# A transformer block: query and key rows packed two heads to a load, written to DRAM once and repeated by 18 small transfers a quad

## What is computed

```
x = x + attn(layernorm(x), w_attn, w_proj, embk, embv)
q, k, v = split(x @ w_attn)                      # 16 heads, d = 8
rel = tril(idx[:, None] - idx[None, :]);  rk = embk[rel];  rv = embv[rel]
att = einsum('bhtd,bhsd->bhts', q, k) / sqrt(d) + einsum('bhtd,tsd->bhts', q, rk)
att = softmax(where(causal, att, -inf))
y = einsum('bhts,bhsd->bhtd', att, v) + einsum('bhts,tsd->bhtd', att, rv)
x = x + y @ w_proj
x = x + moe_ffn(layernorm(x), ...)
```

## Time and profile before

| | |
|---|---|
| median of 3 runs | 943.62 us (940.1 to 944.53) |
| profiled execution, its own time | 949.27 us |
| its span | 947.7 us |
| PE, DVE, ACT, POOL busy | 76%, 64%, 56%, 28% |
| granted TensorE clock, mean | 0.923 |
| first stage, to the first exponential | 111.84 us |
| DMA | 141.37 MB, 149 GB/s mean |

### The profile page before, as it was taken

One profiled execution on the slowest core, in us unless ns is written; L12 is line 12 of the kernel. 1 busy time (PEld: TensorE's weight loads), 2 busy tenths in 40 slices (PEclk: granted clock), 3 DMA queues, 4 the chain that ended last, 5 costly groups with the idle time before them and its releaser, 6 DMA issues. The chain is left out here.

```text
span 947.7 us, 27167 instructions
## 1 busy us (share of the span) xinstructions
PE 717.4 (76%) x10380; PEld 513.2 (54%) x10380; DVE 605.8 (64%) x1930; ACT 529.3 (56%) x1106; POOL 262.4 (28%) x252
## 2 busy tenths in 40 slices
PE   3552277787777887787887787888319999799997
PEld 2331155566565665665666655666216666466664
DVE  4822267685767685766686767777245767647776
ACT  3442278676768575767586777776064334243342
POOL 9411044343334442334452335443000000000000
PEclk9766599999999899999899999999659999999999
DMA  9598758767658776668767659642320000000000
GB/s 303 187 259 255 200 178 267 207 174 206 179 186 263 206 191 177 169 188 241 229 189 193 184 177 262 202 146 74 88 91 1 12 12 12 12 1 11 11 11 11
DMA packets 115675, 141.37 MB, mean 149 GB/s; under 512 B 7088, under 2 KB 81248, under 8 KB 115552
## 3 DMA queue, kind: packets, MB, share of 16 engines
q1 hardware_dynamic: 115552, 139.72, 50.4%
HBM read 82.81 MB, written 56.89 MB: 147 GB/s over the span
## 5 line engine op out<-in xcount | busy, mean ns | idle before, releaser
L801 ACT ACTIVATE work<-ps,nmin 128x128 f32<-128x128 f32 (+3 forms) x512 | 250.0, 537 | 135.2 <-DVE nmin L862 101.3
L862 DVE CUSTOM_DVE_ANT_0 ps<-ps,near 128x128 f32<-128x128 f32 (+3 forms) x512 | 242.5, 509 | 91.7 <-PE ps L683 63.5
L695 PE MATMUL ps<-ident,work 128*128 128x128 f32 x1280 | 213.6, 286 | 80.5 <-ACT work L790 75.4
L695 PEld LDWEIGHTS ps<-ident,work 128*128 128x128 f32 x1280 | 142.3, 144 | 118.3 <-ACT work L790 103.0
L847 DVE COPY work<-ps 128x512 f32<-128x512 f32 (+1 forms) x192 | 123.4, 643 | 86.7 <-PE ps L695 78.5
L683 PE MATMUL ps<-qkb 128*128 128x128 bf16 (+3 forms) x512 | 129.3, 305 | 35.2 <-ACT work L801 32.0
L652 POOL TENSOR_SCALAR_AFFINE_SELECT work<-work 128x512 f32<-128x512 f32 x96 | 61.1, 636 | 330.2 <-ACT work L790 314.0
L656 POOL TENSOR_TENSOR work<-work 128x512 f32<-128x512 f32 x96 | 124.5, 1297 | 8.0
L1219 ACT ACTIVATE silu<-h_ps 128x512 f32<-128x512 f32 x80 | 47.8, 597 | 134.3 <-PE h_ps L1182 134.1
L1194 PEld LDWEIGHTS y_ps<-w_sb,hT 128*128 128x128 f32 x640 | 82.6, 191 | 35.4 <-issue 30.6
L712 PE MATMUL ps<-work,vb 128*9 128x128 f32 x2560 | 96.2, 278 | 6.7 <-ACT relS L779 6.0
(11 more groups left out here) (104 smaller groups left out, 690.8 us busy)
## 6 DMA issues: line engine op xcount, KB each, us to landing
near<-w_slots SPq DMA_DIRECT2D x96, 512.0 KB, 4.6
w_slots<-relS SPq DMA_DIRECT2D x128, 256.0 KB, 4.3
qk_rows<-work SPq DMA_DIRECT2D x48, 256.0 KB, 4.4
qkb<-qk_rows SPq DMA_DIRECT2D x32, 384.0 KB, 5.7
near<-w_slots SPq DMA_DIRECT2D x32, 256.0 KB, 5.0
w_slots<-near SPq DMA_DIRECT2D x8, 512.0 KB, 5.8
v_dram<-work SPq DMA_DIRECT2D x4, 576.0 KB, 6.1
vb<-v_dram SPq DMA_DIRECT2D x4, 576.0 KB, 5.8
```

The costliest lines, as they stand in the source:

```text
L695: ins = nc.tensor.transpose(tp_ps[:, m % 2, n * P:(n + 1) * P], prob[:, m % PROBS, n * P:(n + 1) * P], ident[:, :])
L801: ins = nc.scalar.activation(prob[:, m % PROBS, h * wide:(h + 1) * wide], qk_ps[:, m % 3, h * wide:(h + 1) * wide], ACT.Exp, bias=nmin[:, ...
L862: nc.vector.tensor_tensor_reduce(out=scores, in0=scores, in1=near[:, q % NEAR, a, 4 * P - wide:4 * P, r], scale=1.0, scalar=3e38, op0=ALU. ...
```

## The change

The parts are written once each: `qk_rows` has 3 entries, 6 transfers a group in place of 12. The tile `qkb` becomes two: `qb` (a column block for each head; even heads have their 48 rows on partitions 0 to 47, odd heads on 64 to 111, zeros elsewhere) and `kb` (one column block for a pair of heads, one head in each half). A head's product takes its `qb` against the pair's `kb`. `load_qk` repeats the parts: for each of the two sides 3 transfers for q (24, 16 and 8 partitions) and 6 for k (8 partitions each), all of 2 heads x 1 KB a partition: 18 a quad, 384 KB in all as before.

In the first stage the groups overlap: PE turns the next group ahead of the values of this one, the values go to banks of their own (`value_banks`), ACT copies the next group's turned rows early, layernorm statistics are `bn_stats`/`bn_aggr` for three groups ahead. Group 0's values stay on the chip. Five of eight masks are issued later, quads 4 to 7 are loaded before the rows of group 2, and `wait_rows` moves from ACT's and SP's way into the main loop to the first use of the memory in question (SP's `load_v`, POOL's second row tile, ACT's first `av_copy`).

```diff
-Q_PART = [0, 0, 1, 1, 2, 0]
-K_PART = [0, 1, 0, 1, 0, 2]
+Q_PART = [0, 1, 2, 0, 1, 0]
+K_PART = [0, 0, 0, 1, 1, 2]
+PARTS = 3
+REPEATS = [(0, 3), (3, 2), (5, 1)]
 NPART = len(Q_PART)
 KR = D * NPART
+BASE = [0, P // 2]
+LOADS = len(BASE) * (len(REPEATS) + NPART)
...
+STAGE = PROBS * T + 8 * T + 4 * P + 2 * P * NH
+WORK = STAGE + 6 * GB * NI * P
...
-    NOUT = 2 * NPART + 1
+    NOUT = [2 * PARTS + (g > 0) for g in range(G)]
...
-        for n in range(WSLOTS):
+
+    def masks(sp, lot):
+        for n in lot:
             sp.dma_start(w_slots[n].rearrange("p a c h -> p a (c h)"),
                          t["near"][:, 0, :, 2 * P:4 * P, :].rearrange("p a c h -> p a (c h)")
                          ).then_inc(mask_out, 16)
 
     def sync_rows(sp, g):
-        for n, part_of in enumerate((Q_PART, K_PART)):
+        for n in range(2):
             sp.wait_ge(p3_done, 2 * g + 1 + n)
-            for r, m in enumerate(part_of):
-                dst = qk_rows[r, :, :, g * GB:(g + 1) * GB, n, :].rearrange("d h b t -> (d h) b t")
+            for m in range(PARTS):
+                dst = qk_rows[m, :, :, g * GB:(g + 1) * GB, n, :].rearrange("d h b t -> (d h) b t")
                 sp.dma_start(dst, parts[:, g % 2, n, m, :].rearrange("p (b t) -> p b t", b=GB)
                              ).then_inc(out_done[g % 2], 16)
+        if g == 0:
+            return
         sp.wait_ge(vg_done, g + 1)
         sp.dma_start(v_dram[:, g * GT:(g + 1) * GT, :],
-                     vg[:, g % 2, :, :, :].rearrange("p n h d -> p n (h d)")).then_inc(out_done[g % 2], 16)
+                     values(g).rearrange("p n h d -> p n (h d)")).then_inc(out_done[g % 2], 16)
...
-        nc.gpsimd.memset(t["qkb"][:, :, :, :].bitcast(F32), 0.0)
+        nc.gpsimd.memset(t["qb"][:, :, :].bitcast(F32), 0.0)
...
+    def value_banks(g):
+
+        return ps[:, 5:7, :] if g + 1 < G else ps[:, 2:8:5, :]
+
+    def tensor_turn(pe, g):
         if g == 0:
             wait(pe, id_done, 2)
             pe.wait_ge(w_in, 16)
         pe.wait_ge(xn_done, g + 1)
-        wait(pe, vg_done, g)
+        wait(pe, xnT_done, 2 * g)
         for n in range(GT):
             ins = nc.tensor.transpose(xT_ps[:, n // 4, (n % 4) * P:(n % 4 + 1) * P], xs[:, g * GT + n, :],
                                       t["ident"][:, :])
             if n % 4 == 3:
                 ins.then_inc(xT_ready, 1)
-        wait(pe, xnT_done, 2 * g + 2)
-        wait(pe, rest_done, 2 * g)
+
+    def tensor_rows(pe, g):
+        wait(pe, rest_done, 2 * g - 1)
         for n in range(2):
+            pe.wait_ge(xnT_done, 2 * g + 1 + n)
             nc.tensor.matmul(q_ps[:, n, :], w_sb[:, 0:C], xnT[:, g % 2, n * 512:(n + 1) * 512],
                              start=True, stop=True).then_inc(q_ready, 1)
+        wait(pe, k32_done, g)
         for n in range(2):
             nc.tensor.matmul(k_ps[:, n, :], w_sb[:, C:2 * C], xnT[:, g % 2, n * 512:(n + 1) * 512],
                              start=True, stop=True).then_inc(k_ready, 1)
+
+    def tensor_values(pe, g):
+        wait(pe, vg_done, g)
         for n in range(GT):
-            ins = nc.tensor.matmul(v_ps[:, n // 4, (n % 4) * P:(n % 4 + 1) * P], xnT[:, g % 2, n * P:(n + 1) * P],
-                                   w_sb[:, 2 * C:3 * C], start=True, stop=True)
+            ins = nc.tensor.matmul(value_banks(g)[:, n // 4, (n % 4) * P:(n % 4 + 1) * P],
+                                   xnT[:, g % 2, n * P:(n + 1) * P], w_sb[:, 2 * C:3 * C], start=True, stop=True)
         ins.then_inc(v_ready, 1)
+
+    def tensor_program(pe, early):
+        tensor_turn(pe, 0)
+        for g in range(G):
+            tensor_rows(pe, g)
+            if g + 1 < G:
+                tensor_turn(pe, g + 1)
+            tensor_values(pe, g)
+            if g == G - 2:
+                wait(pe, vg_done, G - 1)
+                early(pe)
...
+            if g + 1 < G:
+                copy_turned(g + 1)
...
-            nc.vector.tensor_reduce(stat[:, 0, lot], xs[:, lot, :], AX.X, ALU.add).then_inc(sum_done, 1)
-            dve.wait_ge(sum_done, g + 1)
-            nc.vector.scalar_tensor_tensor(out=xs[:, lot, :], in0=stat[:, 0, lot].unsqueeze(2).to_broadcast([P, GT, C]),
-                                           scalar=-1.0 / C, in1=xs[:, lot, :], op0=ALU.mult,
-                                           op1=ALU.add).then_inc(xc_done, 1)
-            dve.wait_ge(sq_done, g + 1)
-            nc.vector.tensor_reduce(stat[:, 2, lot], sq[:, :, :], AX.X, ALU.add).then_inc(ssq_done, 1)
+            for n in range(GT):
+                nc.vector.bn_stats(moments[:, n, :], xs[:, g * GT + n, :]).then_inc(mom_done, 1)
+            for n in range(GT):
+                dve.wait_ge(mom_done, GT * g + n + 1)
+                nc.vector.bn_aggr(mv[:, g * GT + n, :], moments[:, n, :]).then_inc(mv_done, 1)
             dve.wait_ge(sd_done, g + 1)
-            nc.vector.reciprocal(rstd[:, lot], stat[:, 4, lot]).then_inc(rstd_done, 1)
+            nc.vector.reciprocal(rstd[:, lot], sd[:, lot]).then_inc(rstd_done, 1)
             dve.wait_ge(rstd_done, g + 1)
-            dve.wait_ge(xc_done, g + 1)
-            nc.vector.tensor_tensor(xs[:, lot, :], xs[:, lot, :],
-                                    rstd[:, lot].unsqueeze(2).to_broadcast([P, GT, C]),
-                                    ALU.mult).then_inc(xn_done, 1)
+            for n in range(GT):
+                k = g * GT + n
+                ins = nc.vector.tensor_scalar(xs[:, k, :], xs[:, k, :], mv[:, k, 0:1], rstd[:, k:k + 1],
+                                              ALU.subtract, ALU.mult)
+            ins.then_inc(xn_done, 1)
...
+        nc.vector.memset(t["kb"][:, :, :].bitcast(F32), 0.0).then_inc(kb_done, 1)
...
-                    src = qk_rows[:, :, h:h + 4, g * GB + b, :, :].rearrange("r d h k t -> (r d) h (k t)")
-                    dst = qkb[0:KR, 4 * u:4 * u + 4, :, :].rearrange("p h k t -> p h (k t)")
-                    sp.dma_start(dst, src).then_inc(qkb_in[u], 16)
+                    for side, base in enumerate(BASE):
+                        src = qk_rows[:, :, h + side:h + 4:2, g * GB + b, :, :]
+                        for r, times in REPEATS:
+                            sp.dma_start(qb[base + r * D:base + (r + times) * D, 4 * u + side:4 * u + 4:2, :],
+                                         src[0:times, :, :, 0, :].rearrange("r d h t -> (r d) h t")).then_inc(qkb_in[u], 16)
+                        for r, m in enumerate(K_PART):
+                            sp.dma_start(kb[base + r * D:base + (r + 1) * D, 2 * u:2 * u + 2, :],
+                                         src[m, :, :, 1, :]).then_inc(qkb_in[u], 16)
...
+                first["masks"](sp, range(3))
                 first["rows"](sp, 0)
-                first["rows"](sp, 1)
-                sp.wait_ge(*first["cleared"])
+                for signal in first["cleared"]:
+                    sp.wait_ge(*signal)
                 sp.wait_ge(*first["first_rows"])
                 for u in range(4):
                     load_qk(0, u)
-                load_v(0)
+                first["rows"](sp, 1)
+                first["masks"](sp, range(3, WSLOTS))
+                for u in range(4, QUADS):
+                    load_qk(0, u)
                 first["rows"](sp, 2)
-                sp.wait_ge(*first["masks_out"])
+                sp.wait_ge(*first["masks_out"](3))
                 for q in range(NQ):
                     if REL_AT[q] == 0:
                         put_rel(q)
                         if q:
                             get_near(q - 1)
                 get_near(REL_AT.count(0) - 1)
-                for u in range(4, QUADS):
-                    load_qk(0, u)
                 first["rows"](sp, 3)
-                first["wait_rows"](sp)
+                sp.wait_ge(*first["masks_out"](WSLOTS))
...
+                            if q == 0:
+                                first["wait_rows"](sp)
...
+                    if q == QUADS:
+                        first["wait_rows"](pool)
...
-                        pe.wait_ge(qkb_in[u], 16 * (e // NI + 1))
+                        pe.wait_ge(qkb_in[u], 16 * LOADS * (e // NI + 1))
...
-                                               qkb[:, n, 0, i * P:(i + 1) * P], qkb[:, n, 1, 0:wide],
+                                               qb[:, n, i * P:(i + 1) * P], kb[:, n // 2, 0:wide],
...
+                    if n == 0:
+                        first["wait_rows"](act)
...
-                first["wait_rows"](act)
...
-    qk_rows = nc.dram_tensor("qk_rows", [NPART, D, H, B, 2, T], BF16, kind="Internal").ap()
+    qk_rows = nc.dram_tensor("qk_rows", [PARTS, D, H, B, 2, T], BF16, kind="Internal").ap()
...
-             "qkb": sb("qkb", [P, NH, 2, T], BF16),
+             "qb": sb("qb", [P, NH, T], BF16),
+             "kb": sb("kb", [P, NH // 2, T], BF16),
```

(27 more changed lines are left out.)

84 lines of the change are left out of this document (41 added, 43 removed).

## The result

| | before | changed |
|---|---|---|
| median | 944.08 us (4 runs) | 1014.61 us (4 runs) |
| ratio | | 1.0747, 95% interval 1.0698 to 1.0796 |
| span of the profiled execution | 947.7 us | 1012.7 us |

The trace of the kernel before is of an execution of 949.27 us, 5 us above this median, the changed kernel's of one of 1014.31: times read from the two traces side by side differ by some 5 us less than the medians do.

The account below looks back on a forecast made before the run. No engine was full; SP's in-order transfer queue was taken to bound the changed kernel. 949.27 + 22 (first stage) + 84.4 (loading stretches) = 1055.7 us, 1050 on the median's scale; forecast 1010 to 1085 (0.56), range 970 to 1110.

Parts of the forecast that it names:

- three loading stretches: Main-loop stretches loading the next group: 9.51 us a quad, losses 28.0, 27.5 and 28.9 us, together 84.4 us.
- c: SP's cost for one small load issue, taken as 0.47 us; each 0.01 us moves the result by 5.8 us.
- my lower bound: SP's small issue from below: 0.35 us, the old load's minimum of 0.303 with 0.05 of gap.
- rival A: Small issues on SP somewhat cheaper, 0.30 to 0.40 us each: still slower, 955 to 1010 us; chance 0.20.
- The signs that I had named: Changed profile: 576 issues of some 0.42 us, about 250 us of SP, first exponential near 130, quads 9.5 us, PE 69%.
- The other part of a quad: In a loading stretch, SP's `get_near`, `put_rel` and gaps beside the 18 issues: 1.05 us a quad.
- my own formula: First loading stretch: quads of 18c + 1.05 from 202.69 put the eighth `get_near` at 278.7 against 250.7, loss 28.0 us.
- The first stage: Before the main loop: loads start at 35.5, first exponential +18.5, three ready units +1, quad 3 +2.4; 22 us.
- SP's queue covers them: Overlapped groups, `bn_stats` and POOL's shorter clearing costed at nothing; without that cover, group rows come out some us sooner.
- C (faster): SP's queue never bounds and ACT's removed 30 us wait comes through; 927 us at c = 0.2; chance 0.07.
- B (dearer): Small issues over 0.53 us, as 8-partition transfers may wait for the DMA engines: over 1085 us; chance 0.14.
- The figure of some 50 ns: Rule against c: at 0.05 us the loads would cost nothing in the loop, the whole near 905 us.

Follow-up runs that it names:

- the other form: Changed kernel with the layernorm's last step made by scalar_tensor_tensor (scalar and broadcast row) in place of the two-scalar tensor_scalar: 1006.46 us, ratio 1.067.
- the first experiment: Changed kernel with parts again written once per row group (12 writes a group) and 4 transfers a quad: 938.35 us, ratio 0.9946 to the kernel before.

## Why the prediction was right, and where its sizes were off

**The mechanism** stood as forecast: SP's queue, with the loss at the first exponential and in exactly the three loading stretches, DVE waiting for `near`, little given back later. A queue with 18 issues in place of one costs nothing until it passes what the engines need for a quad, and everything above.

**c was too high.** I took 0.47 us from the two smallest transfers of the trace. Measured are 0.349 in the first stage, which is my lower bound, in the third stretch 0.368, and in the first two 0.39: from 221.50 to 279.55 the seven loads with their gaps take 7.02 us on average, 18 of them. Those two transfers were small in bytes only, with 48 partitions each; the new ones have 8 to 24. The traces tell more than I had looked for: an issue's duration goes with the transfer issued just ahead of it. The median is 0.299 us behind one of 8 partitions, 0.316 behind one of 16, 0.358 behind one of 24. The k transfer of 48 partitions and 96 KB is the same in two of my kernels; with 8 transfers a quad it stands behind one of 8 partitions, with 4 a quad behind one of 48:

```profile
L595 SPq DMA_DIRECT2D kb<-qk_rows x64: 312/312/1742, 45.1 to 522.0; - x64
L594 SPq DMA_DIRECT2D kb<-qk_rows x64: 303/432/1635, 46.8 to 517.8; - x64
```

My two neighbours stood behind transfers of 48 partitions themselves. No run tried this by itself. The one recorded issue of 0.303 was the better neighbour, and it had been given to rival A. The c that was measured is thus rival A's (0.30 to 0.40), and the 1014.61 us lie in my own band of 1010 to 1085 only because two other terms were too low, which is luck: A's time of 981 for c = 0.35 all through misses by the next two points. The signs that I had named came weaker too: small issues of 0.30 to 0.34 us for 0.42, 193 us of SP for 250, the first exponential at 118.66 for 130, 8.48 us a quad for 9.5, PE's share 73% for 69%.

**The other part of a quad was too cheap.** I priced `get_near`, `put_rel` and gaps at 1.05 us, `put_rel` by its median of 0.37. Where SP is never idle it takes 0.55, as the earlier trace rows already showed in the busy stretch (0.56); together 1.23. With 7.02 + 1.23 = 8.25 my own formula gives 202.69 + 7.02 + 7 x 8.25 + 1.0 = 268.5, less 250.7, 17.8 us for the first stretch; measured 20.2, 18.2 and 16.9. In the first the last read-back also took 6.02 us to land where I had 4.6. The forecast had 28.0, 27.5, 28.9.

**The first stage** was forecast at +22 and came to +11. With 0.349 my sum gives 22 - 144 x 0.121 = 4.6. The rest is the DVE stall that I had costed at nothing ("SP's queue covers them"): the rows of group 0 went out at 35.54 (28.06 with the other form) and the loads started at 41.64 in place of my 35.5, in front of the whole queue, where SP waited for the parts and covered nothing. These 6.1 us and the 4.6 make 10.7. The kernel with the other form stands at +3.9. I had named what hides DVE's work without asking who stands ahead of the queue's start.

**The rivals.** C (faster) would have needed issues under 0.29 us; the shortest of 576 took 0.264, but the mean did not come near. B (dearer) did not occur, and `rel` waited for its load only once, 6 us in the first stage, where it cost nothing. All of the change but the repeated loads, the overlapped groups among it, is worth 4.5 us by the medians of the first experiment, with an interval of 0.1 to 1%; its parts were not tried singly, and with 18 transfers that gain is invisible.

The figure of some 50 ns for the dispatch of a transfer (the Trainium skill, "DMA: Bandwidth & Descriptors", "Anatomy of one DMA") stands there for the GpSimd path and does not hold for these issues on SP: the runs show 0.344 to 0.39 us.

## What to carry to other kernels

Count transfers per queue as work: 0.35 to 0.39 us of the issuing engine each here, the same for 8 and for 16 KB, and compare it with the period of the loop in which they stand; 4 or 8 of them a quad, below that period, were free, and of 18 and 30, above it, each further one was paid by all engines. Saving DRAM writes by more, smaller loads moved work from DMA engines that were not full in the loop to the queue that already handed out every position score. When a queue is forecast to cover something, ask who feeds its first entry.

## What the runs showed of the hardware that I had not expected

DVE's two-scalar form on float32 in SBUF does not run beside POOL's clearing: 9.97 us for eight instead of 2.14, done only after both clearings (19.0), while the form with a scalar and a second tensor takes 2.19 beside the same clearing. The Trainium skill, "SBUF — State Buffer", section "Who interferes with whom", says that `tensor_scalar` can enter a two-port mode which needs the port pair shared with GpSimd, and that whoever issues later blocks fully; the runs agree, in the direction DVE after POOL. That the form was in such a mode no run shows: left alone, the two forms take as long, 2.14 and 2.19 us.

How long SP is taken by one small issue goes with the transfer issued just before it, not with its own bytes. Where the loads were spread over more slots, the same 8-partition k transfer has a median of 0.299 us behind another of its kind, 0.358 behind `put_rel` and 0.496 behind `get_near`; with half the bytes the medians are the same (0.298, 0.356, 0.316 for the three of q, 0.299 for k).

The cost of an issue rises from 0.349 us in the first stage to 0.39 in the first two stretches and 0.368 in the third. Much of that is a few long issues: in the first stretch nine of 144 took over 0.5 us, the longest 1.32, and hold 4.7 us together beyond 0.3 each; in all of the loop's 432 five took 1 us or more (up to 1.77). Halving the bytes did not remove them. What they wait for stays open; no run tried the loop without the position scores' own transfers.
